# A graph layer's expert stage: final rows stored in node order, token gathers of one half row, scatters that add

## The chip, the cores and the metric
The kernel runs on one core of a Trainium2 chip. The metric is the device time of one execution in microseconds (us); the median of three runs of the kernel before is 795.6 us (794.12 to 796.25). All tensors are float32 unless a name says otherwise.

## The reference, cut to what matters
There are 3125 nodes with 256 features and 50000 edges sorted by destination. The function is one layer:

```python
xn = _layernorm(x)
x = x + _L0_gnn_ref(xn, src, dst, edge_type_8, ...) + _L0_mix_ref(xn[None], ...)[0]
x = x + _L0_ffn_ref(_layernorm(x)[None], ...)[0]
```

`_L0_gnn_ref` sums, for every node, the products of its edges' source rows with one of 8 relation matrices (each a mix of 4 bases), adds a loop product, applies GELU and a layer norm. `_L0_mix_ref` is a linear attention over all nodes. `_L0_ffn_ref` is a mixture of 32 experts with one expert per token:

```python
idx = jnp.argmax(logits, axis=-1)
h = relu(einsum('nd,ndh->nh', xf, W1[idx]) + b1[idx])      # 256 -> 64
out = relu(einsum('nh,nhd->nd', h, W2[idx]) + b2[idx])     # 64 -> 256
```

So each node has two rows of 256 numbers that the last stage needs: the row x after the first two parts (call it x2), and its normalised form, which the router and the experts read. The result is x2 plus the expert's output.

## The kernel before, in words
The nodes stand in NT = 25 tiles of 128 rows (the last has 53). Edges are worked in 49 "octets" of 8 x 128 edges. For each 128 edges GpSimd issues an indirect DMA (L534) that gathers 128 source rows of 1 KB from DRAM; TensorE multiplies them with a window matrix (L786), VectorE adds the products to an accumulator in SBUF (L1189). This is the edge stage, up to about 623 us. Its order is written out by hand in `edge_schedule`, and beside the later octets the node tiles are finished one by one (early and product on TensorE, gelu on ScalarE, first_stats, second_stats, finish_row and route on VectorE). `rowbuf` has three slots, and in each slot a tile's normalised rows lie in the first 256 columns and its x2 rows in the last 256.

`store_row(t)` on SyncE's queue (L409) waits until tile t's rows are ready (x2n_made) and stores the 512 columns to the DRAM tensor `rows_d` with one DMA. A slot is written again by tile t+3, for which VectorE waits on `stored`. On the same queue stand the loads of x (L404), the load of the experts' first weights (L413, L414) before the last tile's store, and that of the second weights (L418) after it.

The tail, after the last tile, is this. VectorE and TensorE sort the tokens by expert: `inv_i` gives for each place in sorted order the node that stands there (L1386 to L1436), and a table of NPAIR = 56 pairs (expert, token tile) says which tile each expert has tokens in. Then:
- GpSimd waits for all row stores and for inv_i, and issues 25 indirect gathers (L559), one for each tile of sorted tokens: 128 rows of 2 KB from `rows_d` into `token`, both halves.
- TensorE works in groups of 4 pairs, 14 groups. `hidden(g)` (L1025) is the first product, `turn_tiles(g + 1)` (L1015) transposes the next four token tiles once each has landed (f_in), `outer(g - 1)` (L1034) is the second product of the group before.
- ScalarE copies the four experts' weights of a group (load_w1, L711), applies ReLU to the hidden product once f_hid says it is there (L729), and copies the transposed tiles out of PSUM once f_turned says so (keep_turned, L718). hidden(g + 1) waits for these copies (f_xt).
- VectorE folds each pair's output into the tile's place in `f_ys` (L1482, one instruction a pair, counted by f_y). From pair 31 on, tile t = p - 31 is complete; `finish(t)` adds the gathered x2 half (L1473) and counts f_rows.
- GpSimd waits for f_rows and scatters the tile's 128 rows of 1 KB to `out` with an indirect DMA (L564). The last thing waited for is f_stored, all 25 scatters (SyncE).

A branch that is taken only for unusual edge lists (`redo`) repeats the work in a slower way; it isn't taken here.

Of the kernel before, what the change touches and what calls it, by code (L numbers as in the profile page):

```python
# [22 lines left out]
P = 128  # L23
N, D, E = 3125, 256, 50000
R, B, X, H = 8, 4, 32, 64
# [36 lines left out]
ALU = mybir.AluOpType  # L62
ACT = mybir.ActivationFunctionType
AX = mybir.AxisListType
F32, BF16 = mybir.dt.float32, mybir.dt.bfloat16
# [3 lines left out]
def rows(t):  # L69

    return P if t < NT - 1 else LAST
# [31 lines left out]
def gps_layer(nc, x, src_t, type_rows, dst_t, dst_rows, basis, comp, loop_w, h_bias, ln_gamma, ln_beta,  # L103
              w_qk, b_qk, w_v, b_v, bn_gamma, bn_beta, router_w, router_b, w1_t, b1_t, w2_t, relation_of,
              group_mask, out):
    with ExitStack() as ctx:
# [3 lines left out]
        def sem(name):  # L110
            return ctx.enter_context(nc.semaphore(name))
# [1 line left out]

        xn_d = nc.dram_tensor("xn_d", [N, D], F32).ap()
        bounds_d = nc.dram_tensor("bounds_d", [2, NWIN], I32).ap()
        rows_d = nc.dram_tensor("rows_d", [N, 2 * D], F32).ap()


        acc_raw = sb("acc_raw", [P, KD * B * NPAD])
# [6 lines left out]
        token = both[:, :].rearrange("p (t f) -> p t f", f=ROW)  # L126
# [70 lines left out]
        rowbuf = xn_raw[:, 8 * D:14 * D].rearrange("p (j f) -> p j f", j=3)  # L197
# [113 lines left out]
        once, again = Chain("once", v_own), Chain("again", Tally(sem("again_own")))  # L311
# [9 lines left out]
        f_in = [sem(f"f_in{s}") for s in range(NT)]  # L321
# [3 lines left out]
        f_relu = sem("f_relu")  # L325
        f_out = sem("f_out")
        f_y = sem("f_y")
        f_rows = sem("f_rows")
        f_w1 = sem("f_w1")
        f_stored = sem("f_stored")  # L330

# [38 lines left out]
        f_ys = acc_raw[:, at:at + NT * D]  # L370
# [35 lines left out]
        def store_row(eng, t, c):  # L406

            eng.wait_ge(c.x2n_made, t + 1)
            eng.dma_start(rows_d[t * P:t * P + rows(t), :], rowbuf[0:rows(t), t % 3, :]).then_inc(c.stored[t % 3], 16)  # L409

        def load_first(eng, done):

# [7 lines left out]
        def stores_of(j):  # L420

            return len(range(j, NT, 3))
# [72 lines left out]
        @block.gpsimd  # L495
        def _(pool):
            g = nc.gpsimd

            p_own.mark(g.memset(ident[:, :], 0.0))
            p_own.mark(g.memset(identb[:, :], 0.0))  # L500
            p_own.mark(g.memset(before[:, :], 1.0))
            g.memset(onesb[:, :], 1.0).then_inc(consts_made, 1)
            g.memset(ones_pp[:, :], 1.0).then_inc(consts_made, 1)
            at = p_own.mark(g.iota(part_i[:, :], pattern=[[0, 1]], base=0, channel_multiplier=1))
            pool.wait_ge(p_own.sem, at)
            g.tensor_copy(part_col[:, :], part_i[:, :]).then_inc(part_made, 1)
            at = p_own.mark(g.iota(iota_i[:, :], pattern=[[1, P]], base=0, channel_multiplier=0))
            for first, n, count in runs_of_reach():
                w = OCT // PAIR
                ins = g.iota(reach[:, first * w:(first + n) * w], pattern=[[P, n], [0, w]], base=P * count, channel_multiplier=0)  # L510
                p_own.mark(ins)
            pool.wait_ge(p_own.sem, p_own.at)
            pool.sem_inc(consts_made, 1)
            pool.wait_ge(p_own.sem, at)
            g.affine_select(out=ident[:, :], in_=ident[:, :], compare_op=ALU.not_equal, fill=1.0, base=0,
                            pattern=[[-1, P]], channel_multiplier=1).then_inc(consts_made, 1)
            g.affine_select(out=identb[:, :], in_=identb[:, :], compare_op=ALU.not_equal, fill=1.0, base=0,
                            pattern=[[-1, P]], channel_multiplier=1).then_inc(consts_made, 1)
            g.affine_select(out=before[:, :], in_=before[:, :], compare_op=ALU.is_gt, fill=0.0, base=0,
                            pattern=[[1, P]], channel_multiplier=-1).then_inc(consts_made, 1)  # L520
            g.tensor_copy(iota_b[:, :], iota_i[:, :]).then_inc(part_made, 1)
            pool.wait_ge(part_made, 2)
            g.tensor_copy(iota[:, :], iota_i[:, :]).then_inc(consts_made, 1)

            g.memset(acc_raw[:, TC * P:], 0.0).then_inc(acc_zeroed, 1)

            pool.wait_ge(xn_stored, 16 * (GROUPS + 1))
            pool.wait_ge(tables_loaded, 32)
            pool.wait_ge(rel_ready, 1)

            def octet(q, beside, i):
                for k in range(OCT):
                    pool.wait_ge(multiplied, OCT * q + k + 1)
                    g.indirect_dma_start(gath[:, k, :], None, xn_d,  # L534
                                         bass.IndirectOffsetOnAxis(ap=src_i[:, OCT * q + k:OCT * q + k + 1], axis=0)).then_inc(gathered[k], 16)

            edge_schedule(octet)


            pool.wait_ge(flag_ready, 1)  # L540
            redo = pool.value_load(flag[0:1, 0:1], min_val=0, max_val=1)
            with pool.If(redo > 0):
                with pool.Fori(0, NOCT * OCT) as t:
                    pool.wait_ge(slow_step, (2 * NT + 2) * t + 1)
                    g.tensor_copy(idx_st[:, 0:1], src_i[:, ds(t, 1)]).then_inc(slow_idx, 1)
                    pool.wait_ge(slow_idx, t + 1)
                    pool.sem_inc(slow_seen, 1)
                    g.indirect_dma_start(gath[:, 0, :], None, xn_d,
                                         bass.IndirectOffsetOnAxis(ap=idx_st[:, 0:1], axis=0)).then_inc(slow_gath, 16)
                    pool.wait_ge(slow_gath, 16 * t + 16)  # L550
                for j in range(3):
                    pool.wait_ge(again.stored[j], 16 * stores_of(j))

            for j in range(3):
                pool.wait_ge(once.stored[j], 16 * stores_of(j))
            pool.wait_ge(inv_ready, 1)
            for t in range(NT):
                n = rows(t)
                g.indirect_dma_start(token[0:n, t, 0:2 * D], None, rows_d,  # L559
                                     bass.IndirectOffsetOnAxis(ap=inv_i[0:n, t:t + 1], axis=0)).then_inc(f_in[t], 16)  # L560
            for t in range(NT):
                n = rows(t)
                pool.wait_ge(f_rows, t + 1)
                g.indirect_dma_start(out, bass.IndirectOffsetOnAxis(ap=inv_i[0:n, t:t + 1], axis=0),  # L564
                                     f_ys[0:n, t * D:(t + 1) * D], None).then_inc(f_stored, 16)


        @block.scalar
# [508 lines left out]
        def _(v):  # L1077
# [121 lines left out]
            def first_stats(t, c):  # L1199

                n = rows(t)
                v.wait_ge(c.gelu_done, t + 1)
                at = c.own.mark(d.bn_stats(stat_a[0:n, :], h[0:n, t % 2, :]))
                v.wait_ge(c.x_in[t % 3], 16 * (t // 3 + 1))
                if t >= 3:
                    v.wait_ge(c.stored[t % 3], 16 * (t // 3))
                c.own.mark(d.tensor_tensor(rowbuf[0:n, t % 3, D:2 * D], ps_mix[t % 2][0:n, D:2 * D], xr[0:n, t % 3, :], ALU.add))
                v.wait_ge(c.own.sem, at)
                d.bn_aggr(mv_a[0:n, :], stat_a[0:n, :]).then_inc(c.var_a, 1)
                v.wait_ge(c.var_a, t + 1)  # L1210
                d.scalar_tensor_tensor(y[0:n, :], h[0:n, t % 2, :], mv_a[0:n, 0:1], gam_bc[0:n, :], ALU.subtract, ALU.mult).then_inc(c.y_made, 1)
# [169 lines left out]
            def rank_and_experts(o):  # L1381
# [84 lines left out]

                d.memset(f_ys.bitcast(BF16), 0.0).then_inc(y_zeroed, 1)

                def finish(t):
                    n = rows(t)  # L1470
                    place = f_ys[0:n, t * D:(t + 1) * D]
                    v.wait_ge(f_in[t], 16)
                    d.tensor_tensor(place, place, token[0:n, t, D:2 * D], ALU.add).then_inc(f_rows, 1)  # L1473

                for g in range(NPAIR // FT):
                    tiles = row_values(v, pair_i[0:1, 1, FT * g:FT * (g + 1)], NT - 1, CLAMPED)
                    for f in range(FT):
                        p = FT * g + f
                        v.wait_ge(f_out, FT * g + f // 2 * 2 + 2)
                        v.wait_ge(f_y, p) if p > 0 else v.wait_ge(y_zeroed, 1)  # L1480
                        place = f_ys[:, ds(tiles[f] * D, D)]
                        d.scalar_tensor_tensor(place, ps[g % 2 * 2 + f // 2][:, f % 2 * D:(f % 2 + 1) * D], limit[:, p:p + 1], place, ALU.min, ALU.max).then_inc(f_y, 1)  # L1482
                        if p >= X - 1:
                            v.wait_ge(f_y, p + 1)
                            finish(p - X + 1)

            with v.If(redo < 1):
                rank_and_experts(v_own)
# [4 lines left out]
            with v.If(redo > 0):  # L1493
# [3 lines left out]
                v.wait_ge(ffn_loaded, 32)  # L1497
                v.wait_ge(w2_loaded, 16)
                for j in range(3):
                    v.wait_ge(once.stored[j], 16 * stores_of(j))  # L1500
                d.memset(acc_raw[:, :].bitcast(BF16), 0.0).then_inc(zero_again, 1)
                v.wait_ge(zero_again, 1)
                v.sem_inc(slow_step, 1)
# [78 lines left out]
```

## Time and profile before
| | us |
|---|---|
| median of 3 runs | 795.6 |
| profiled execution, its own time | 790.61 |
| its span in the trace | 788.7 |
| TensorE busy | 585.8 (74%) |
| VectorE busy | 386.3 (49%) |
| GpSimd busy | 458.2 (58%) |
| ScalarE busy | 163.5 (21%) |

One execution was recorded. PE is TensorE's matmuls, PEld its weight loads, DVE VectorE, ACT ScalarE, POOL GpSimd, SP SyncE; a q behind a name means that engine's instruction queue. "idle before <- X" is how long the engine had nothing to do before this group, and X is who ended it; "remote" stands where the profile finds no instruction that raised the awaited signal just then. The ends of matmuls are modelled. Numbers after a line's name are microseconds from the span's start, unless a column says ns.

### The profile page before, as it was taken

Reading aid. Unit: us, or ns where it says so; the run is one execution under the profiler, and the core shown is the slowest. Engines: PE = TensorE matmul, PEld = TensorE weight load, DVE = VectorE, ACT = ScalarE, POOL = GpSimd, SP = SyncE. Lnnn points to the kernel's source line nnn. Section 1 sums busy time; section 2 is a strip of 40 time slices with the busy share of each in tenths; the row PEclk is TensorE's granted clock in tenths of the full one; section 3 lists DMA queues with packets and bytes.
Section 4 is the critical chain, followed back from the end, with each engine's and each line's share of the span. In section 5 each row is a group of like instructions: output and inputs, shape, how many; then the busy total and the mean of one; then the engine's idle time right before and its main releaser. Section 6 shows DMA issues by size and latency. Waiting matters only on the chain.

```text
span 788.7 us, 10440 instructions
## 1 busy us (share of the span) xinstructions
PE 585.8 (74%) x3181; PEld 471.6 (60%) x3181; DVE 386.3 (49%) x1272; ACT 163.5 (21%) x345; POOL 458.2 (58%) x464
## 2 busy tenths in 40 slices
PE   0366686888888768698999798897979982419980
PEld 0356675666665647477777666775858741318860
DVE  2844445333322334446666646456547677303552
ACT  0450000000000001022332312132122350115520
POOL 9146676666666666566676667666666400740165
PEclk9969999898999998699999888899989995559986
DMA  8563333333333344234434433334334326640021
GB/s 227 157 185 88 87 99 88 90 89 91 93 91 94 91 141 121 68 94 126 123 115 131 126 112 115 103 114 128 110 108 130 108 99 166 200 126 2 15 81 72
DMA packets 41872, 86.78 MB, mean 110 GB/s; under 512 B 11280, under 2 KB 23378, under 8 KB 41491
## 3 DMA queue, kind: packets, MB, share of 16 engines
q0 software_dynamic: 22576, 61.01, 26.7%
q1 hardware_dynamic: 18372, 22.95, 9.4%
q10 hardware_dynamic: 864, 2.08, 1.1%
q8 instruction: 29, 0.48, 0.2%
q14 instruction: 31, 0.25, 0.1%
HBM read 73.21 MB, written 12.80 MB: 109 GB/s over the span
## 4 chain that ended last, share of the span: by engine, by line
PE 56%; another core or an unknown queue 14%; DVE 10%; issue 7%; DMA 4%; POOL 3%; ACT 2%; SPq 1%; DVEq 0%; ACTq 0%; POOLq 0%
PE ps L786 23%; PE ps L828 11%; PE ps L817 6%; PE ps L1025 3%; PE ps L1034 2%; PE ps L793 2%; DMA both<-in_x 2%; PE ps L800 2%; POOL gath L534 2%; PE ps L805 2%; DMA gath<-xn_d,src_i 1%; POOL out L564 1%; PE ps L850 1%; PE ps L840 1%
## 5 line engine op out<-in xcount | busy, mean ns | idle before, releaser
L534 POOL DMA_INDIRECT gath<-xn_d,src_i x392 | 386.5, 986 | 214.9 <-issue 90.9
L786 PE MATMUL ps<-wmat,gath 128*128 128x144 f32 x1568 | 257.8, 309 | 25.5 <-DMA gath<-xn_d,src_i 10.7
L786 PEld LDWEIGHTS ps<-wmat,gath 128*128 128x128 f32 x1568 | 229.4, 203 | 50.8 <-issue 22.4
L1189 DVE TENSOR_TENSOR acc_raw<-acc_raw,ps 128x144 f32 x392 | 101.8, 300 | 283.2 <-PE ps L786 203.5
L1162 DVE TENSOR_TENSOR wmat<-hit,wts 128x576 f32<-128x576 f32 x100 | 75.3, 753 | 0.3
L564 POOL DMA_INDIRECT out<-acc_raw,inv_i x25 | 25.4, 1015 | 55.5 <-DVE acc_raw L1473 49.1
L1482 DVE SCALAR_TENSOR_TENSOR acc_raw<-ps,wts,acc_raw 128x256 f32 x56 | 27.0, 482 | 59.7 <-PE ps L1034 46.6
L559 POOL DMA_INDIRECT both<-rows_d,inv_i x25 | 24.3, 971 | 52.6 <-DVE inv_i L1436 45.2
L828 PE MATMUL ps<-wk_et,acc_raw 128*128 128x256 f32 (+1 forms) x200 | 53.1, 391 | 0.0
L828 PE MATMUL ps<-wq_wv,acc_raw 128*128 128x256 f32 (+1 forms) x200 | 52.6, 388 | 0.0
L817 PE MATMUL ps<-cmat,both 128*128 128x512 f32 (+1 forms) x100 | 52.5, 651 | 0.0
L1025 PE MATMUL ps<-acc_raw,gath 128*64 x224 | 33.3, 308 | 24.9 <-ACT acc_raw L718 22.7
L1025 PEld LDWEIGHTS ps<-acc_raw,gath 128*64 128x64 f32 x224 | 28.8, 156 | 30.7 <-issue 30.7
L793 PE MATMUL ps<-both,wk_et 128*128 128x256 f32 (+1 forms) x104 | 29.9, 414 | 18.4 <-DVE top L1197 18.4
L828 PEld LDWEIGHTS ps<-wq_wv,acc_raw 128*128 128x128 f32 (+1 forms) x200 | 36.9, 193 | 4.8 <-issue 0.2
L805 PE MATMUL ps<-both,wk_et 128*128 128x257 f32 (+1 forms) x100 | 28.5, 410 | 14.8 <-ACT wk_et L621 7.8
L828 PEld LDWEIGHTS ps<-wk_et,acc_raw 128*128 128x128 f32 (+1 forms) x200 | 35.1, 194 | 3.6 <-issue 0.2
L621 ACT ACTIVATE wk_et<-ps 128x256 f32<-128x256 f32 x24 | 9.2, 384 | 126.9 <-remote 71.3
L840 PE MATMUL ps<-ident,both 128*128 128x128 f32 (+1 forms) x50 | 11.2, 308 | 31.4 <-issue 16.4
L750 PE MATMUL ps<-ident,both 128*128 128x128 f32 x50 | 10.8, 387 | 31.6 <-DVEq L1116 23.7
L793 PEld LDWEIGHTS ps<-both,wk_et 128*128 128x128 f32 x104 | 19.6, 210 | 21.8 <-DVE top L1197 19.6
L646 ACT ACT_TABLE_LOAD x25 | 32.1, 1283 | 0.5
(194 smaller groups left out, 619.7 us busy)
## 6 DMA issues: line engine op xcount, KB each, us to landing
gath<-xn_d,src_i POOLq DMA_INDIRECT x392
rows_d<-both SPq DMA_DIRECT2D x24, 256.0 KB
both<-in_x SPq DMA_DIRECT2D x24, 128.0 KB
both<-in_x SPq DMA_DIRECT2D x4, 640.0 KB, 17.2
xn_d<-both SPq DMA_DIRECT2D x4, 640.0 KB
acc_raw<-in_w_t SPq DMA_DIRECT2D x1, 2080.0 KB
acc_raw<-in_w_t SPq DMA_DIRECT2D x1, 2048.0 KB, 7.5
acc_raw<-in_type_rows ACTq DMA_DIRECT2D x1, 1600.0 KB, 15.6
```

The lines of the kernel that those rows point to most:

```text
L534: g.indirect_dma_start(gath[:, k, :], None, xn_d, bass.IndirectOffsetOnAxis(ap=src_i[:, OCT * q + k:OCT * q + k + 1], axis=0)).then_inc(ga ...
L564: g.indirect_dma_start(out, bass.IndirectOffsetOnAxis(ap=inv_i[0:n, t:t + 1], axis=0), f_ys[0:n, t * D:(t + 1) * D], None).then_inc(f_stor ...
L646: s.activation(h[0:n, t % 2, :], ps_mix[t % 2][0:n, 0:D], ACT.Gelu).then_inc(c.gelu_done, 1)
L786: ins = t_.matmul(ps_edge[quarter][:, m * B * WIN:(m + 1) * B * WIN], gath[:, k, m * P:(m + 1) * P], wmat[:, k, :, :].rearrange("p b w -> ...
L793: ins = t_.matmul(ps_mix[m][:, 0:n], wk[:, k, m * P:(m + 1) * P], xnt[:, k, ds(first, n)], start=k == 0, stop=k == KD - 1)
L805: ins = t_.matmul(ps_sum[m][:, 0:D + 1], et[0:n, j, m * P:(m + 1) * P], tile, start=start, stop=stop)
L817: t_.matmul(bank, xnt[:, k, P * t:P * t + n], cmat[:, k, :], start=k == 0, stop=False)
L828: ins = t_.matmul(ps_mix[t % 2][0:n, 0:D], acc[:, f, t * P:t * P + n], basis_sb[m][:, b, :], start=False, stop=f == KD * B - 1, skip_group ...
L1025: ins = t_.matmul(ps[4 + g % 2][0:H, f * P:(f + 1) * P], f_w[:, g % 2, f, k * H:(k + 1) * H], xts[:, ds(tiles[f] * D + k * P, P)], start=k ...
L1162: d.tensor_tensor(wmat[:, half * w:half * w + w, :, :], hit[:, :, :].unsqueeze(2).to_broadcast([P, w, B, WIN]), wts[:, :, cut].rearrange(" ...
L1189: d.tensor_tensor(place, place, ps_edge[w][:, m * B * WIN:(m + 1) * B * WIN].rearrange("p (b w) -> p b w", w=WIN), ALU.add).then_inc(added, 1)
L1482: d.scalar_tensor_tensor(place, ps[g % 2 * 2 + f // 2][:, f % 2 * D:(f % 2 + 1) * D], limit[:, p:p + 1], place, ALU.min, ALU.max).then_inc ...
```

## The change
Each tile is stored with two DMAs: the normalised half to `rows_d`, which now has 256 columns, and the x2 half straight to its node rows of `out`. The gathers fetch only the normalised half, 1 KB a row. VectorE's finish is gone, and the scatter of tile t waits for f_y >= t + 32 (the fold of pair t + 31). The scatter is an accumulating DMA: it adds the rows of `f_ys` to what lies in `out`. The waits on `stored` count 32 a tile, as two DMAs raise it by 16 each.

```diff
-        rows_d = nc.dram_tensor("rows_d", [N, 2 * D], F32).ap()
+        rows_d = nc.dram_tensor("rows_d", [N, D], F32).ap()
...
             eng.wait_ge(c.x2n_made, t + 1)
-            eng.dma_start(rows_d[t * P:t * P + rows(t), :], rowbuf[0:rows(t), t % 3, :]).then_inc(c.stored[t % 3], 16)
+            eng.dma_start(rows_d[t * P:t * P + rows(t), :], rowbuf[0:rows(t), t % 3, 0:D]).then_inc(c.stored[t % 3], 16)
+            eng.dma_start(out[t * P:t * P + rows(t), :], rowbuf[0:rows(t), t % 3, D:2 * D]).then_inc(c.stored[t % 3], 16)
...
             for j in range(3):
-                pool.wait_ge(once.stored[j], 16 * stores_of(j))
+                pool.wait_ge(once.stored[j], 32 * stores_of(j))
             pool.wait_ge(inv_ready, 1)
             for t in range(NT):
                 n = rows(t)
-                g.indirect_dma_start(token[0:n, t, 0:2 * D], None, rows_d,
+                g.indirect_dma_start(token[0:n, t, 0:D], None, rows_d,
                                      bass.IndirectOffsetOnAxis(ap=inv_i[0:n, t:t + 1], axis=0)).then_inc(f_in[t], 16)
             for t in range(NT):
                 n = rows(t)
-                pool.wait_ge(f_rows, t + 1)
+                pool.wait_ge(f_y, t + X)
                 g.indirect_dma_start(out, bass.IndirectOffsetOnAxis(ap=inv_i[0:n, t:t + 1], axis=0),
-                                     f_ys[0:n, t * D:(t + 1) * D], None).then_inc(f_stored, 16)
+                                     f_ys[0:n, t * D:(t + 1) * D], None, compute_op=ALU.add).then_inc(f_stored, 16)
...
                 if t >= 3:
-                    v.wait_ge(c.stored[t % 3], 16 * (t // 3))
+                    v.wait_ge(c.stored[t % 3], 32 * (t // 3))
...
-                def finish(t):
-                    n = rows(t)
-                    place = f_ys[0:n, t * D:(t + 1) * D]
-                    v.wait_ge(f_in[t], 16)
-                    d.tensor_tensor(place, place, token[0:n, t, D:2 * D], ALU.add).then_inc(f_rows, 1)
...
                         d.scalar_tensor_tensor(place, ps[g % 2 * 2 + f // 2][:, f % 2 * D:(f % 2 + 1) * D], limit[:, p:p + 1], place, ALU.min, ALU.max).then_inc(f_y, 1)
-                        if p >= X - 1:
-                            v.wait_ge(f_y, p + 1)
-                            finish(p - X + 1)
```

## Rows read from the trace of the kernel before
**Rows 1.** Busy time by stretch, core 0: microseconds and counts; last clock, DMA share, GB/s.
```profile
102.00:600.00 498.00, 412.97 (x2197) 332.01 (x2196) 241.15 (x841) 85.48 (x142) 333.68 (x338) 0.92 0.36 107
671.00:701.00 30.00, 9.11 (x34) 6.64 (x34) 7.25 (x7) 3.89 (x14) 22.99 (x24) 0.56 0.72 206
712.00:745.00 33.00, 33.00 (x219) 27.70 (x217) 15.48 (x32) 17.71 (x68) 0.00 (x0) 1.00 0.01 1
761.40:782.30 20.90, 8.97 (x37) 7.07 (x35) 11.50 (x27) 1.68 (x7) 16.28 (x16) 0.66 0.24 97
783.30:785.80 2.50, 0.00 (x0) 0.00 (x0) 0.00 (x0) 0.00 (x0) 0.00 (x0) 0.50 0.08 21
```
**Rows 2.** Chain of waits, end of the kernel: start, length, what.
```profile
678.88 18.28 another core or an unknown queue
```
**Rows 3.** Timeline while the tokens are gathered: start, length, engine, line, idle before.
```profile
652.33 0.24 SPq L409 DMA_DIRECT2D rows_d<-both  x1
...
669.75 0.94 POOL L559 DMA_INDIRECT both<-rows_d,inv_i  x1 [45.25 <-DVE inv_i L1436]
...
679.03 3.67 PE L1025 MATMUL ps<-acc_raw,gath 128*64 x16 [1.11 <-ACT acc_raw L718]
...
682.63 1.97 PE L1015 MATMUL ps<-ident,both 128*128 128x128 f32 x8
...
697.28 1.12 ACT L729 ACTIVATE gath<-ps,acc_raw 64x128 f32<-64x128 f32 x4 [18.40 <-remote]
...
704.93 1.07 ACT L718 COPY acc_raw<-ps 128x512 f32<-128x512 f32 x2 [6.53 <-remote]
...
706.15 3.67 PE L1025 MATMUL ps<-acc_raw,gath 128*64 x16 [21.56 <-ACT acc_raw L718]
```
**Rows 4.** Timeline after the gathers, while GpSimd is silent.
```profile
713.56 1.96 PE L1025 MATMUL ps<-acc_raw,gath 128*64 x16
...
715.66 1.12 ACT L729 ACTIVATE gath<-ps,acc_raw 64x128 f32<-64x128 f32 x4 [2.46 <-PE ps L1025]
...
716.38 1.89 PE L1034 MATMUL ps<-acc_raw,gath 65*128 x8
...
718.21 1.96 PE L1025 MATMUL ps<-acc_raw,gath 128*64 x16
```
**Rows 5.** The two indirect transfers of the tail: shortest, median, longest in ns.
```profile
L559 POOL DMA_INDIRECT both<-rows_d,inv_i x25: 942/947/1573, 669.7 to 699.8; - x25
...
L564 POOL DMA_INDIRECT out<-acc_raw,inv_i x25: 967/972/1557, 745.7 to 780.7; - x25
```
**Rows 6.** Timeline of the scatters.
```profile
745.01 0.42 DVE L1473 TENSOR_TENSOR acc_raw<-acc_raw,both 128x256 f32<-128x256 f32 x1
...
745.71 1.03 POOL L564 DMA_INDIRECT out<-acc_raw,inv_i  x1 [44.37 <-DVE acc_raw L1473]
...
752.53 1.99 PE L1034 MATMUL ps<-acc_raw,gath 65*128 x8
...
759.13 0.48 DVE L1482 SCALAR_TENSOR_TENSOR acc_raw<-ps,wts,acc_raw 128x256 f32 x1 [4.09 <-remote]
...
759.54 3.60 PE L1034 MATMUL ps<-acc_raw,gath 65*128 x8 [0.19 <-ACT gath L729]
...
761.38 0.97 POOL L564 DMA_INDIRECT out<-acc_raw,inv_i  x1 [3.79 <-DVE acc_raw L1473]
...
766.65 3.72 PE L1034 MATMUL ps<-acc_raw,gath 65*128 x16
...
776.47 0.48 DVE L1482 SCALAR_TENSOR_TENSOR acc_raw<-ps,wts,acc_raw 128x256 f32 x1 [3.00 <-remote]
...
780.69 1.56 POOL L564 DMA_INDIRECT out<-acc_raw,inv_i  x1 [0.30 <-issue]
```
**Rows 7.** Who waited for whom, edge stage: total, times, longest.
```profile
DVE acc_raw L1189 <- PE ps L786: 187.8, 88, 5.9
...
DVE acc_raw L1189 <- remote: 59.5, 29, 3.6
```

More of the change, by code:

```diff
@@ L327, in gps_layer @@
         f_y = sem("f_y")
-        f_rows = sem("f_rows")
         f_w1 = sem("f_w1")
@@ L551, in _ @@
                 for j in range(3):
-                    pool.wait_ge(again.stored[j], 16 * stores_of(j))
+                    pool.wait_ge(again.stored[j], 32 * stores_of(j))
             for j in range(3):
-                pool.wait_ge(once.stored[j], 16 * stores_of(j))
+                pool.wait_ge(once.stored[j], 32 * stores_of(j))
             pool.wait_ge(inv_ready, 1)
@@ L1499, in _ @@
                 for j in range(3):
-                    v.wait_ge(once.stored[j], 16 * stores_of(j))
+                    v.wait_ge(once.stored[j], 32 * stores_of(j))
                 d.memset(acc_raw[:, :].bitcast(BF16), 0.0).then_inc(zero_again, 1)
```

## The prediction, on record before the changed kernel ran
> **What bounds the kernel now.** I read the page's slices first: in the tail the DMA digits are high while TensorE is nearly idle. Then busy time by stretch. The edge stage is TensorE's (413 of 498 us busy), and the change leaves its instructions alone. From 671 to 701 us TensorE is busy for 9 us of 30, GpSimd for 23, and the DMA engines move 206 GB/s at a share of 0.72: this is the gather of the tokens. From 712 to 745 us TensorE is busy all the time at the full granted clock (1.0, 2.4 GHz). From 761.4 to 782.3 us GpSimd's scatters fill the stretch (16.3 of 20.9 us busy) [rows 1].
>
> The chain of waits has one link of 18.28 us from 678.88, called unknown [rows 2]. In the timeline it is ScalarE, which starts the ReLU of group 0 at 697.28 after 18.40 us of idle, though TensorE's hidden(0) stands as ended at 682.70 and the transposes behind it at 684.60. A second wait ends at 704.93 with the copies out of PSUM, for transposes that also ended at 684.60. So TensorE's signals arrive 14.6 and up to 20.3 us late, and hidden(1) starts only at 706.15 [rows 3]. With GpSimd silent there is no such lag: hidden(2) ends at 715.52 and its ReLU starts at 715.66 [rows 4]. While GpSimd scatters there is one again, but shorter: the outer product ends at 754.52 and VectorE's fold starts at 759.13; the one that ends at 770.37 is folded at 776.47 [rows 6]. In the edge stage, with 1 KB gathers at most times, VectorE's longest idle before its additions is 5.9 us, and 3.6 where nothing else explains it [rows 7]; that bounds a lag there from above, for the idle holds true waiting too. I read this as: TensorE's completion signals are held back while indirect DMAs run, for 3 to 6 us where rows have 1 KB, for 15 to 20 us where they have 2 KB. That the size of the row makes the difference is the assumption of this forecast; the number of DMAs in a row would be another reading.
>
> **The change, part by part.**
>
> *Two stores for one.* SyncE issues one more DMA a tile; the last store's issue took 0.24 us at 652.33. The bytes are the same. All stores must have landed before the first gather, which starts at 669.75 and waits for inv_i [rows 3]: 17 us of cover. The weights' loads behind them slip by one issue, some 0.3 us, against first uses past 670 us. The slots' second use is three tiles later. I take 0. Were the cover gone, it would cost the landing of one store.
>
> *Gathers of 1 KB.* The issue is not cheaper: 947 ns for 2 KB rows, and 972 ns for the 1 KB rows of the scatter [rows 5]. 25 of them at 0.947 + 0.30 of gap fill 31 us, as now. A tile can't be there earlier than now by more than its shorter transfer, and tile t is issued at 669.75 + 1.25 t. What changes is the traffic: 206 GB/s would halve to about 103, near the 107 of the edge stage and the 97 of the scatters [rows 1]. So I give TensorE's signals a lag of 4 us in place of 14.6 (between 3.6 and 5.9 of [rows 7]). Then: ReLU of group 0 at 682.7 + 4 = 686.7; it takes 1.12, the copies behind it 1.22 until hidden starts (704.93 to 706.15): hidden(1) at 689.0. It takes 3.67, the transposes 1.97 [rows 3]. f_hid arrives at 692.7 + 4 = 696.7, and with 1.12 + 1.22 hidden(2) starts at 699.0, TensorE's own work (3.67 + 1.97 + 3.60 for the outer product at the lower clock [rows 6]) ending at 698.3. Then 3.67 + 1.97 + 3.60 again: hidden(3) at 708.3. Now it starts at 718.21 [rows 4]. That is 9.9 us, less a little because the granted clock rose to 1.0 only by 712 and may be late again: I take -9.5. Bounds: 0, if the lag stays until the gathers end; -14.7, if there is none (hidden(1) at 685.0, then two times 9.24: hidden(3) at 703.5, and the clock may well be up earlier, so up to -16).
>
> A rule of the Trainium skill speaks against this. "DMA: Bandwidth & Descriptors", section "Anatomy of one DMA — SWDGE (gpsimd) path", gives a transfer issued by GpSimd about 2 us of fixed cost plus bytes over 436 GB/s, so 1 KB rows save 0.3 us of a gather and nothing of its issue. By it this part would be worth 0.3 us; what it leaves out is the lag of TensorE's signals that the rows show.
>
> *finish is gone.* The first scatter waits now for a fold and a finish of 0.42 us that starts at 745.01; it starts at 745.71 [rows 6]. -0.4. The other 24 are hidden behind GpSimd's stream.
>
> *Scatters that add.* Now: 745.71 to 782.25 (780.69 + 1.56) are 36.5 us for 25 issues; at 0.972 + 0.30 with the longer last one they would be 32.4, and the rest is the gap of 3.79 us before 761.38, a late signal [rows 5, 6]. No row shows an accumulating DMA. From below: the plain scatter, 972 ns. From above: the 1557 ns of the longest of these issues, and, further off, twice the plain one, 1.94 us, if every row needs a second address worked out. I take +0.2 us an issue, nearer to the plain row, since the index and the row count are the same: +5.0 over 25, of which the gap absorbs 1.8 (nine slower scatters come later to it): +3.2. Bounds 0 and +14.9 - 3.8 = +11 (1557 ns), +24.4 - 3.8 = +20.6 (1.94 us). Behind the last issue the trace has 6.45 us to the end of the span, in 2.5 of which the DMA share is 0.08, a little over one engine of 16 (0.0625) [rows 1]: the 53 rows of the last tile go through one engine. If the add needs a second read for each row, these 2.5 us may double. +2.0, bounds 0 and +2.5. The other scatters' transfers have room: a share of 0.24 in the stream [rows 1].
>
> "Collectives: The Full Stack", section "The bandwidth ceiling: the fold count and why AG ≠ RS ≠ AR", of the Trainium skill says that an add in the DMA path costs two source reads and two reading descriptors a chunk, which halved the rate there. By it the last tile would pay all of its 2.5 us, and GpSimd would have half as many descriptors more to write, 1.46 us an issue for 0.972: +12.2 - 3.8 = +8.4 for the stream. No run here shows it.
>
> *Sum* against the profiled execution: 0 - 9.5 - 0.4 + 3.2 + 2.0 = -4.7, so a span of 784.0 and a time of 785.9. The median of the runs lies 5.0 us above the profiled time; I carry that over: 795.6 - 4.7 = **790.9 us**.
>
> **The rivals.**
> 1. *The signals stay held until the gathers end.* The gathers are as many and as dense as before, and if it is their issue and not their bytes that holds the signals, hidden(1) starts near 704 to 706 as now. For it: the scatters too have 1 KB rows and lags of 4 to 6 us at a share of 0.24. Against: these are a third of 14.6 to 20.3. Price: the -9.5 falls away, +4.8 stays: 800.4 us.
> 2. *GpSimd's scatters become the end*, the other side. The mechanism: an accumulating issue is dear, and from 745 on GpSimd's stream is what ends last, so each 0.1 us costs 2.5. At 1557 ns: -9.9 + 11.1 + 2.5 = +3.7, 799.3 us; at 1.94 us: -9.9 + 20.6 + 2.5 = +13.2, 808.8 us. It decides from where 25 e - 3.8 + 2.5 exceeds 9.9, e = 0.45: an issue of 1.42 us. For it: the stream is full already. Against: issues of the same row count cost the same for one and two KB and for both directions.
> 3. *No lag and a plain price.* TensorE follows the gathers, and the scatter costs as now: -14.7 - 0.4 = -15.1, 780.5 us. For it: the lag in the edge stage is short most of the time.
>
> **How the numbers follow.** Forecast 0.43 (its own range 786 to 796), rival 1 0.22, rival 2 0.20, rival 3 0.15. About 0.3% (2.4 us) is what a measurement of this kernel can tell from no change. Faster: 0.36 of the forecast, all of rival 3, 0.03 of rival 1, 0.01 of rival 2: 0.55. Slower: 0.15 of rival 1, 0.17 of rival 2, 0.02 of the forecast: 0.34. The same: 0.11. Range 781 to 806: it leaves out half of rival 3 and the dear end of rival 2.
>
> **What would show it.** Right: ReLU of group 0 within 6 us of hidden(0)'s end, hidden(3) at 705 to 711, a DMA share near 0.4 in the gathers; L564 at 1.0 to 1.35 us; 7 to 9 us from the last issue to the end. Wrong: the 18.4 us idle before L729 still there (rival 1); L564 at 1.4 us or more and no gap left in its stream (rival 2). A wait on `stored` that ends after inv_i would make the two stores dear; I see none.

## The result: 810.9 us, 2% slower, and outside the range

The changed kernel took 810.86 us (median of 4 runs, 808.19 to 813.27), the kernel before 795.13 us on the same chip (794.12 to 796.25): a ratio of 1.0197, 95% interval 1.016 to 1.0233. The forecast was 790.9 us, the range 781 to 806.

The two profiled executions lie at opposite ends of what the runs show: before at 790.61 with a median of 795.13, after at 813.27 with a median of 810.86. So the traces differ by 22.7 us and the timed runs by 15.7. A part of the trace's difference, 9.5 us, is already there when the first gather starts (669.75 before, 679.26 after), ahead of everything that the prediction priced but the two stores; in two later profiles of the same pair (e5, e6 below) the last gathers are 1.2 us apart (698.90 and 697.68). The stretches are therefore measured from the first gather.

The tail of the changed kernel. The chain of waits, its links from 687.15 on that are over 2 us long (start, length, what):
```profile
687.15 21.04 issue
709.42 5.16 another core or an unknown queue x2
715.79 3.67 PE ps L1025 x16
799.71 2.75 POOL out L564
```
The same stretch in the timeline (start, length, engine, line, idle before):
```profile
679.26 0.94 POOL L559 DMA_INDIRECT both<-rows_d,inv_i  x1 [44.95 <-DVE inv_i L1436]
...
687.30 3.67 PE L1025 MATMUL ps<-acc_raw,gath 128*64 x16 [0.83 <-ACT acc_raw L718]
...
690.90 1.13 PE L1015 MATMUL ps<-ident,both 128*128 128x128 f32 x8
...
708.30 1.12 ACT L729 ACTIVATE gath<-ps,acc_raw 64x128 f32<-64x128 f32 x4 [21.14 <-issue]
709.21 1.57 POOL L559 DMA_INDIRECT both<-rows_d,inv_i  x1 [0.30 <-issue]
714.57 1.07 ACT L718 COPY acc_raw<-ps 128x512 f32<-128x512 f32 x2 [5.15 <-remote]
715.79 3.67 PE L1025 MATMUL ps<-acc_raw,gath 128*64 x16 [23.77 <-ACT acc_raw L718]
...
754.96 1.65 POOL L564 DMA_INDIRECT out<-acc_raw,inv_i  x1 [44.18 <-DVE acc_raw L1476]
...
756.91 1.58 POOL L564 DMA_INDIRECT out<-acc_raw,inv_i  x1 [0.31 <-issue]
...
799.71 2.75 POOL L564 DMA_INDIRECT out<-acc_raw,inv_i  x1 [0.30 <-issue]
```
This answers to [rows 3] and [rows 6]. ScalarE is idle for 21.14 us before the ReLU of group 0, where before it was 18.40: hidden(0) stands as ended at 690.97 and its signal arrives at 708.30, when GpSimd is about to issue its last gather. Nothing of the expected gain is there. From the first gather to the first scatter it is 75.96 us before and 75.70 after. From the first scatter to the end of the last issue it is 36.5 us before and 47.5 after, and behind that 6.45 and 8.9 us to the end of the span.

The two indirect transfers of the changed kernel (shortest, median, longest in ns), against [rows 5]:
```profile
L559 POOL DMA_INDIRECT both<-rows_d,inv_i x25: 942/944/1572, 679.3 to 709.2; - x25
...
L564 POOL DMA_INDIRECT out<-acc_raw,inv_i x25: 1553/1553/2750, 755.0 to 799.7; - x25
```
Busy time by stretch (as in [rows 1]: PE, PEld, DVE, ACT, POOL busy; clock, DMA share, GB/s): the gathers, the second half of the scatters, and what lies behind the last issue:
```profile
681.00:711.00 30.00, 7.61 (x34) 5.77 (x33) 7.15 (x6) 3.85 (x14) 22.78 (x24) 0.56 0.36 104
771.00:802.40 31.40, 2.58 (x12) 1.92 (x11) 3.87 (x8) 0.18 (x1) 26.52 (x17) 0.59 0.62 70
802.50:805.00 2.50, 0.00 (x0) 0.00 (x0) 0.00 (x0) 0.00 (x0) 0.00 (x0) 0.50 0.21 8
805.00:808.00 3.00, 0.00 (x0) 0.00 (x0) 0.00 (x0) 0.00 (x0) 0.00 (x0) 0.50 0.08 12
```
The traffic of the gathers did halve (206 to 104 GB/s, share 0.72 to 0.36), as the prediction said, and TensorE is no busier for it (7.61 us in 30, before 9.11). The adding scatters keep the DMA engines busier (share 0.62, before 0.24) while they move less (70 GB/s, before 97).

### The profile page after: what moved, and what is told of

Its sections match the earlier page's. It is cut to its first block, busy times and chain, and to the rows that moved or that the text cites. A ratio compares the mean times of both kernels' runs of the same rounds, so it can differ in the third digit from the quotient of the medians.

```text
span 811.4 us, 10414 instructions
## 1 busy us (share of the span) xinstructions
PE 584.2 (72%) x3180; PEld 470.0 (58%) x3181; DVE 377.7 (47%) x1247; ACT 163.6 (20%) x345; POOL 470.6 (58%) x464
## 4 chain that ended last, share of the span: by engine, by line
PE 50%; another core or an unknown queue 17%; issue 11%; DVE 9%; POOL 5%; DMA 3%; ACT 3%; SPq 1%; DVEq 0%; POOLq 0%; ACTq 0%
PE ps L786 19%; PE ps L828 10%; PE ps L817 6%; PE ps L1025 3%; POOL out L564 3%; PE ps L1034 3%; PE ps L793 3%; DMA both<-in_x 2%; POOL gath L534 2%; PE ps L850 1%; PE ps L840 1%; DVE acc_raw L1189 1%; PE ps L818 1%; ACT wk_et L621 1%
## 5 line engine op out<-in xcount | busy, mean ns | idle before, releaser
L786 PE MATMUL ps<-wmat,gath 128*128 128x144 f32 x1568 | 260.9, 310 | 28.6 <-DMA gath<-xn_d,src_i 10.9
L564 POOL DMA_INDIRECT out<-acc_raw,inv_i x25 | 40.2, 1607 | 51.5 <-DVE acc_raw L1476 46.6
L828 PE MATMUL ps<-wk_et,acc_raw 128*128 128x256 f32 (+1 forms) x200 | 51.3, 380 | 0.0
L1025 PE MATMUL ps<-acc_raw,gath 128*64 x224 | 30.9, 297 | 24.6 <-ACT acc_raw L718 24.6
L840 PE MATMUL ps<-ident,both 128*128 128x128 f32 (+1 forms) x50 | 10.9, 302 | 36.5 <-issue 28.0
L658 ACT ACTIVATE both<-both,eps_col 128x1 f32<-128x1 f32 (+1 forms) x25 | 7.4, 295 | 124.7 <-DVE both L1225 75.4
L646 ACT ACT_TABLE_LOAD x25 | 32.1, 1283 | 0.4
L1152 DVE TENSOR_TENSOR hit<-rel,iota 128x144 f32<-128x144 f32 x100 | 30.3, 303 | 3.1 <-ACT wts L599 3.1
```

The source lines that it names most:

```text
L646: s.activation(h[0:n, t % 2, :], ps_mix[t % 2][0:n, 0:D], ACT.Gelu).then_inc(c.gelu_done, 1)
L786: ins = t_.matmul(ps_edge[quarter][:, m * B * WIN:(m + 1) * B * WIN], gath[:, k, m * P:(m + 1) * P], wmat[:, k, :, :].rearrange("p b w -> ...
L828: ins = t_.matmul(ps_mix[t % 2][0:n, 0:D], acc[:, f, t * P:t * P + n], basis_sb[m][:, b, :], start=False, stop=f == KD * B - 1, skip_group ...
L1025: ins = t_.matmul(ps[4 + g % 2][0:H, f * P:(f + 1) * P], f_w[:, g % 2, f, k * H:(k + 1) * H], xts[:, ds(tiles[f] * D + k * P, P)], start=k ...
L1152: d.tensor_tensor(hit[:, :, :], rel[:, cut].unsqueeze(2).to_broadcast([P, w, WIN]), iota[:, 0:WIN].unsqueeze(1).to_broadcast([P, w, WIN]), ...
```

## The experiments

The chips that ran these kernels are of two sorts, and each experiment can only be read with that. The kernel before took 795.1 us on the chip of the first measurement (its number isn't on record), 692.6 on that of e1 to e4, 789.5 (e5 to e8), 692.8 (e9 to e12) and 799.0 (e13 to e15); the last four are different chips. In the traces of the two chips near 692 us TensorE's signals arrive on time ("punctual" below); in those of the others they are late. "Late" is read against the end of the matmuls, which the profile models; the same model gives 0.14 us on a punctual chip (e2), so the difference between chips is real, but whether the matmuls end late or their signals are held can't be seen. Each ratio is to the kernel before on the same chip.

**On a punctual chip.**

*e1, two stores alone.* The kernel before, its row store cut in two DMAs to the same tensor:
```diff
-            eng.dma_start(rows_d[t * P:t * P + rows(t), :], rowbuf[0:rows(t), t % 3, :]).then_inc(c.stored[t % 3], 16)
+            eng.dma_start(rows_d[t * P:t * P + rows(t), 0:D], rowbuf[0:rows(t), t % 3, 0:D]).then_inc(c.stored[t % 3], 16)
+            eng.dma_start(rows_d[t * P:t * P + rows(t), D:2 * D], rowbuf[0:rows(t), t % 3, D:2 * D]).then_inc(c.stored[t % 3], 16)
```


> The kernel before with each tile's row store cut into two DMAs of 1 KB rows (both halves still go to rows_d, gathers, finish and scatters as before). Theory A (the two stores cost nothing, all 15.7 us lie in the tail): 795.1, within 1 us of before. Theory B (they slow the later edge stage, since the profile of the change has its first gather 9.5 us later, of which 3.6 stood before the first store): 797 to 801.

691.22 us, ratio 0.9987 (0.996 to 1.0015). The second store costs nothing that can be measured.

*e2, the change without the add.* Its scatters overwrite, so the x2 half is missing from the output.
```diff
-                                     f_ys[0:n, t * D:(t + 1) * D], None, compute_op=ALU.add).then_inc(f_stored, 16)
+                                     f_ys[0:n, t * D:(t + 1) * D], None).then_inc(f_stored, 16)
```


> The changed kernel with scatters that overwrite instead of adding (the add of x2 is left out). Theory A (the accumulating issue is the whole loss): L564 back at 0.97 us, 8.9 us behind the last issue back to 6.4, late signals in the scatters again, so 13 us faster than the change: 796 to 798. Rival (GpSimd's stream is long for another reason, the two stores or the bytes): 803 or more.

687.25 us, ratio 0.9935 (0.9911 to 0.9959): 5.3 us of gain, and not by way of TensorE's signals. The timeline of e2, hidden(0) and its ReLU:
```profile
601.89 3.67 PE L1025 MATMUL ps<-acc_raw,gath 128*64 x16 [0.83 <-ACT acc_raw L718]
...
605.70 1.12 ACT L729 ACTIVATE gath<-ps,acc_raw 64x128 f32<-64x128 f32 x4 [3.96 <-PE ps L1025]
```
The ReLU starts 0.14 us after hidden(0), though GpSimd issues its gathers just as densely. There is no lag on this chip, and from the first gather (593.82) to the first scatter (645.92) it takes 52.1 us where it took 75.7. What the smaller rows gain here is the wait for the tiles themselves: TensorE's transposes wait for gathered tiles for 5.2 us in all in e1 (2 KB rows) and for 1.1 us in e2, and e1 takes 56.3 us from the first gather to the first scatter.

*e3, pauses in the gathers.* The kernel before with one wait more, so that GpSimd issues 12 gathers and then four at a time, each four once the tiles up to four back are transposed:
```diff
             for t in range(NT):
                 n = rows(t)
+                if t >= 3 * FT and t % FT == 0:
+                    pool.wait_ge(f_turned, t - FT)
```


> The kernel before, with GpSimd's gathers paced: tiles 12, 16, 20 and 24 each wait until TensorE's transposes of all but the four tiles before them are counted. Theory I (an unbroken run of GpSimd's indirect DMAs holds TensorE's signals, whatever their bytes; a pause lets them out): the 18.4 us idle before L729 shrinks to 3 to 7, group 3's hidden product starts near 708 in place of 718, 785 to 789. Rival (the signals are late for a reason that has nothing to do with the gathers' run, or the gathers' end is what counts): 795, or slower by the pauses, 797.

692.24 us, ratio 1.0013 (0.9985 to 1.0041). Where no signal is late, pauses gain nothing and cost nothing.

*e4, GpSimd silent.* The changed kernel with its gathers replaced by plain loads on SyncE's queue, in node order; the sort is left out of the loads:
```diff
+            sp.wait_ge(inv_ready, 1)
+            for t in range(NT):
+                sp.dma_start(token[0:rows(t), t, 0:D], rows_d[t * P:t * P + rows(t), :]).then_inc(f_in[t], 16)
...
-                g.indirect_dma_start(token[0:n, t, 0:D], None, rows_d,
-                                     bass.IndirectOffsetOnAxis(ap=inv_i[0:n, t:t + 1], axis=0)).then_inc(f_in[t], 16)
```


> The changed kernel with the 25 token loads issued by SyncE as direct DMAs of the same 128 KB, in node order (the sort of the tokens is left out). Theory I (GpSimd's issues hold TensorE's signals): ReLU of group 0 starts within 1 us of its product's end, group 3 starts 15 to 20 us earlier after inv_i, the accumulating scatters stay: 791 to 796. Rival (any DMA traffic into the token buffer holds them): the long idle stays, 809 to 811.

706.05 us, ratio 1.0192 (1.0157 to 1.0227). The change with its own gathers was not run on this chip, so what the loads gain here can't be read from this run; the accumulating scatters (median 1553 ns) make it slower than e2.

**On a chip with late signals (before 789.5 us).**

*e5 and e6, the pair again.* The changed kernel and the kernel before, unaltered.

> The changed kernel once more, beside the kernel before, on the chip of this comparison. Where TensorE's signals are on time (as in the four runs before, 692.6 for the kernel before): the overwriting form was 5.3 us faster than before, the add costs 25 x 0.58 + 2.5 = 17 us, so 704, 12 us slower than before (ratio 1.017). Where they are late: 811 against 795, as first measured. Rival (on such a chip the stream starts so much earlier that the add is covered): ratio under 1.005.

> The kernel before, for its profile on the chip of this comparison. If TensorE's signals are on time: ReLU of group 0 starts within 0.3 us of its product's end, the edge stage ends some 75 us earlier than in the first profile, 690 to 694. If late: 791 to 796 with the 18 us idle before L729.

e5: 804.66 us, ratio 1.0193 (1.0167 to 1.0218), the first result again; e6: 788.07 us. From the timelines, first e5, then e6:
```profile
676.87 3.67 PE L1025 MATMUL ps<-acc_raw,gath 128*64 x16 [0.83 <-ACT acc_raw L718]
...
692.83 1.12 ACT L729 ACTIVATE gath<-ps,acc_raw 64x128 f32<-64x128 f32 x4 [16.10 <-remote]
...
698.90 1.58 POOL L559 DMA_INDIRECT both<-rows_d,inv_i  x1 [0.30 <-issue]
...
742.60 1.65 POOL L564 DMA_INDIRECT out<-acc_raw,inv_i  x1 [42.13 <-DVE acc_raw L1476]
...
787.38 2.75 POOL L564 DMA_INDIRECT out<-acc_raw,inv_i  x1 [0.30 <-issue]
```
```profile
676.98 3.67 PE L1025 MATMUL ps<-acc_raw,gath 128*64 x16 [1.12 <-issue]
...
694.48 1.12 ACT L729 ACTIVATE gath<-ps,acc_raw 64x128 f32<-64x128 f32 x4 [17.65 <-remote]
...
697.68 1.57 POOL L559 DMA_INDIRECT both<-rows_d,inv_i  x1 [0.30 <-issue]
...
743.12 1.02 POOL L564 DMA_INDIRECT out<-acc_raw,inv_i  x1 [43.86 <-DVE acc_raw L1473]
...
778.14 1.56 POOL L564 DMA_INDIRECT out<-acc_raw,inv_i  x1 [0.30 <-issue]
```
The first scatters start within 0.5 us of one another, the last 9.2 us apart. With 1.2 us more for the last issue and 2.5 behind it that is the whole 12.9 us between the spans (786.2 and 799.1). This pair compares the two row sizes on one chip: with half the bytes hidden(0)'s signal is 12.3 us late, with all of them 13.8, and from the first gather to the first scatter it takes 73.7 us in place of 75.4. In both the signal arrives while GpSimd is still issuing (7.6 and 4.8 us before the last gather's issue ends), so it isn't held until the run of issues is over.

*e7, fewer rows to add.* The changed kernel; each accumulating scatter carries at most 64 rows, the other rows are left out:
```diff
             for t in range(NT):
                 n = rows(t)
+                n = min(n, 64)
                 pool.wait_ge(f_y, t + X)
```


> The changed kernel with each accumulating scatter cut to its first 64 rows (the other rows' adds are left out). Theory D (the add costs GpSimd per row, since it writes more for each): L564 falls from 1.55 to 1.0 us or less. Rival (a fixed extra of 0.58 us for an accumulating DMA): L564 at 1.4 to 1.55 us.

803.46 us in one run. The scatters of e7:
```profile
L565 POOL DMA_INDIRECT out<-acc_raw,inv_i x25: 1397/1401/2762, 749.0 to 790.0; - x25
```
Half of the rows take 0.15 us off 1.55, and 64 added rows still cost 0.43 us more than 128 plain ones. The reading that each row's second address makes the price would give 1.26 us (0.972 and half of 0.58). The larger part of the price doesn't go by the rows, then, provided that a plain scatter of 64 rows costs no more than one of 128; that was not run. The last tile's 53 rows are dearest in every version.

*e8, pauses in the kernel before.* The edit of e3.

> The paced gathers of the run before, once more, for a chip on which TensorE's signals are late. There theory I (an unbroken run of GpSimd's DMAs holds them) expects 6 to 10 us less than before and an idle of 3 to 7 us before L729. Where signals are on time, both theories expect no change (ratio 0.998 to 1.003).

775.86 us, ratio **0.9819** (0.9795 to 0.9843): faster than both kernels, by 13.6 us over the kernel before. The timeline of e8 while the tokens are gathered:
```profile
683.71 0.95 POOL L561 DMA_INDIRECT both<-rows_d,inv_i  x1 [0.30 <-issue]
686.97 1.12 ACT L731 ACTIVATE gath<-ps,acc_raw 64x128 f32<-64x128 f32 x4 [7.91 <-remote]
687.27 0.94 POOL L561 DMA_INDIRECT both<-rows_d,inv_i  x1 [2.61 <-remote]
...
689.18 3.67 PE L1027 MATMUL ps<-acc_raw,gath 128*64 x16 [5.09 <-ACT acc_raw L720]
...
691.02 0.95 POOL L561 DMA_INDIRECT both<-rows_d,inv_i  x1 [0.30 <-issue]
...
692.99 1.12 ACT L731 ACTIVATE gath<-ps,acc_raw 64x128 f32<-64x128 f32 x4 [3.16 <-PE ps L1027]
...
707.13 1.57 POOL L561 DMA_INDIRECT both<-rows_d,inv_i  x1 [1.90 <-PE ps L1017]
...
731.57 1.03 POOL L566 DMA_INDIRECT out<-acc_raw,inv_i  x1 [22.87 <-DVE acc_raw L1475]
```
GpSimd stops issuing at 684.66 (683.71 + 0.95); 2.3 us later ScalarE receives TensorE's signal, and 2.6 us later GpSimd. The idle before the ReLU falls from 17.65 to 7.91 us. The last gather is issued 9.5 us later than in e6 (707.13 for 697.68), and the first scatter 11.6 us earlier. The gain is more than was expected (6 to 10 us), though the idle stayed longer than the 3 to 7 us that the expectation had.

**On another punctual chip (before 692.8 us).** These four were meant for late signals, and the chip had none; so e10 and e11 only repeat e2 and e4.

> The changed kernel, with one wait more: before the gathers of tiles 12, 16, 20 and 24 GpSimd waits until the tiles up to four back are transposed, so that its issues come in bursts. Theory (an unbroken run of GpSimd's indirect issues holds TensorE's signals; the bytes of the rows do not matter): where the kernel before takes some 790 us, the pauses give the change the 13.6 us that they gave the kernel before, so about 1.002 of before (1.019 - 0.017): the idle before the ReLU of group 0 falls from 16 to 8 us, first scatter some 11 us earlier. Rival (the gain of the pauses came from the 2 KB rows' traffic, which 1 KB rows do not have): still 1.019. Where TensorE's signals are on time anyway (before near 692 us) both expect 1.019 and nothing is told apart.

The change with the pauses of e3: 705.88 us, ratio 1.0202 (1.0138 to 1.0267). The change without pauses was not run on a punctual chip; e11 below, without GpSimd's gathers, takes the same time.

> The changed kernel without the add (its scatters overwrite, so the x2 half is missing from the output). Theory (bytes of the gathered rows do not matter, the accumulating issue costs 0.58 us more): where signals are late, idle before the ReLU of group 0 is 16 to 18 us as before, first scatter within 1 us of before, ratio 0.995 to 1.000. Rival (bytes do matter, and the first pair of profiles hid it in run-to-run variation): idle of 4 to 8 us and ratio 0.98 to 0.988. Against the change (1.019) both expect the add alone to be worth 15 to 19 us where nothing else changes: 11 of issues, 1.2 of the last issue, 2.5 of landing, and the late-signal gap it covers.

The kernel of e2: 687.38 us, ratio 0.9926 (0.9892 to 0.996). Against e9 that is 18.5 us for the add, more than on a late chip, since here no gap of late signals takes up a part of it.

> The changed kernel with the 25 token gathers replaced by plain loads of 25 x 128 rows in node order on SyncE's queue (the sort by expert is left out, so tokens meet wrong experts; all counts and sizes stay). GpSimd is silent, the bytes and the 25 waits are the same. Theory (GpSimd's issuing holds the signals): ReLU of group 0 starts within 3 us of hidden(0)'s end, first scatter 14 to 17 us earlier than in the change, ratio 1.000 to 1.004 where before is some 790 us. Rival (the transfers' traffic, or something of this place in the program, holds them): idle of 10 us or more remains, ratio 1.012 to 1.019. Where signals are on time: 1.019, as measured once.

The kernel of e4: 705.56 us, ratio 1.0187 (1.0122 to 1.0252).

> The kernel before with pauses that begin one group earlier: the gathers of tiles 8, 12, 16, 20 and 24 wait. Theory: 8 issues in a row in place of 12 (10 us in place of 15), so the idle before the ReLU of group 0 falls from 7.9 to 2 to 4 us; the later groups are bound by their own chain, so 2 to 5 us less than the version that pauses from tile 12: 0.976 to 0.980. Rival (the pauses now starve TensorE of tiles, since each group waits for the last transposes of the one before): 0.982 to 0.988. Where signals are on time: 1.000 to 1.006, the pauses can only cost.

The edit of e3 with `t >= 2 * FT`: 693.29 us, ratio 1.0028 (0.9992 to 1.0064). Whether the earlier pause gains anything where signals are late was not tried.

**On another chip with late signals (before 799.0 us).**

> The changed kernel without the add (the x2 half is missing from the output), once more, since the last chip had TensorE's signals on time. Expected only for a chip where they are late (before some 790 us). Theory (bytes of the gathered rows do not matter): idle of 16 to 18 us before the ReLU of group 0 as in before, first scatter within 1 us of before, ratio 0.995 to 1.000. Rival (bytes do matter): idle of 4 to 8 us and ratio 0.98 to 0.988. On a chip with punctual signals: 0.993, as twice.

The kernel of e2: 797.12 us, ratio 0.9981 (0.9962 to 1.0001). The timeline, and the scatters:
```profile
705.95 1.12 ACT L729 ACTIVATE gath<-ps,acc_raw 64x128 f32<-64x128 f32 x4 [21.23 <-issue]
706.83 1.57 POOL L559 DMA_INDIRECT both<-rows_d,inv_i  x1 [0.30 <-issue]
712.25 1.07 ACT L718 COPY acc_raw<-ps 128x512 f32<-128x512 f32 x2 [5.17 <-remote]
```
```profile
L564 POOL DMA_INDIRECT out<-acc_raw,inv_i x25: 969/974/1560, 752.2 to 787.5; - x25
```
Rows of 1 KB, a plain scatter, and the long idle is there in full. All of the change but the add is worth 1.9 us here, at the edge of what can be told from nothing.

> The changed kernel with the 25 token gathers replaced by plain loads on SyncE's queue in node order (the sort is left out of the loads), once more for a chip with late signals. Theory (GpSimd's issuing holds the signals): ReLU of group 0 starts within 3 us of hidden(0)'s end, first scatter 14 to 17 us earlier than in the change, ratio 1.000 to 1.004. Rival (the traffic or the place in the program): idle of 10 us or more, 1.012 to 1.019. On a chip with punctual signals: 1.019, as twice.

The kernel of e4, GpSimd silent: 787.24 us, ratio **0.9866** (0.9827 to 0.9905), although its scatters cost 1555 ns as in the change. The timeline, and the stretch of the loads:
```profile
675.88 11.58 SPq L496 DMA_DIRECT2D both<-rows_d  x25
...
684.53 3.67 PE L1026 MATMUL ps<-acc_raw,gath 128*64 x16 [0.91 <-ACT acc_raw L719]
...
688.34 1.12 ACT L730 ACTIVATE gath<-ps,acc_raw 64x128 f32<-64x128 f32 x4 [3.96 <-PE ps L1026]
...
690.57 1.96 PE L1026 MATMUL ps<-acc_raw,gath 128*64 x16 [1.34 <-ACT acc_raw L719]
...
695.21 1.96 PE L1026 MATMUL ps<-acc_raw,gath 128*64 x16
```
```profile
677.00:688.00 11.00, 6.52 (x26) 5.34 (x26) 7.88 (x11) 2.66 (x10) 0.00 (x0) 0.50 0.86 257
```
The DMA engines move 257 GB/s at a share of 0.86 (206 and 0.72 in the gathers of the kernel before), and the ReLU starts 0.14 us after hidden(0). So it is not the traffic that makes TensorE's signals late. The loads differ from the gathers in two things, though: SyncE issues them, and they are not indirect. Which of the two frees the signals this run doesn't tell. From the first load to the first scatter (727.50) it takes 51.6 us, in place of 75.7. The expectation (1.000 to 1.004) was too high, in the main because it valued the lag at 14 to 17 us where it is worth 24.

> The changed kernel with pauses before the gathers of tiles 12, 16, 20 and 24, once more for a chip with late signals. Theory (an unbroken run of issues holds the signals): 1.002, idle before the ReLU of group 0 near 8 us. Rival (the pauses helped only because of the 2 KB rows' traffic): 1.019. On a chip with punctual signals: 1.020, as once.

The kernel of e9: 796.22 us, ratio 0.9968 (0.9943 to 0.9993). The pauses take the change from 2% slower to a little faster than before, where 1.002 was expected. The change without them was not run on this chip (1.0193 and 1.0197 in the other two sessions with late signals); against e13, on this chip, the first scatter comes 61.7 us after the first gather in place of 75.5. The idle before its first ReLU:
```profile
693.66 1.12 ACT L731 ACTIVATE gath<-ps,acc_raw 64x128 f32<-64x128 f32 x4 [9.39 <-remote]
```

## Why the prediction was wrong

*Two stores, 0.* Right as far as the runs go: e1 on a punctual chip, and on a late one e13, which has both stores and is no slower than the kernel before. By themselves they were not run on a late chip.

*Gathers of 1 KB, -9.5.* Wrong, and with it the sign of the sum. The step that failed is the assumption that "the size of the row makes the difference": the lag was read off two stages that differ in three things, the rows' size, the traffic and how densely GpSimd issues, and I gave it to the first. The runs took the size apart from the rest: with half the bytes the idle stays (21.14 us in the change, 21.23 in e13, and 16.10 beside 17.65 in e5 and e6, on one chip), with more traffic and no indirect gather of GpSimd it is gone (e14), with the same DMAs in bursts it is more than halved (e8). On these chips the late signals go with GpSimd's dense indirect gathers, 25 in a row at 1.25 us each, whatever their rows' size; whether it is the issuing or the transfers' form, and what lets the signals through before the run is over, stays open. Measured worth of the smaller rows with finish gone: -1.9 us at a late chip (e13), -5.3 and -5.5 at the punctual ones (e2, e10), by the medians. Rival 1 named this and had 0.22; its argument, 25 issues as dense as before, stood in the text. The bound was off too: the whole lag is worth 24 us (75.7 less 51.6), where I had put no more than 16. The step that fell short is the clock: without the lag I had hidden(1) at 685.0, 15.3 us after the first gather (14.7 in e14), but then two groups at 9.24 us each, at the lower clock. In e14 a group takes 4.64 us (690.57 to 695.21) and the granted clock is 1.00 from 688 to 700 us, so hidden(3) comes 9.2 us earlier still.

The rule that I weighed and set aside, in the Trainium skill's "DMA: Bandwidth & Descriptors", section "Anatomy of one DMA — SWDGE (gpsimd) path" (a fixed cost plus a small term for bytes), gave 0.3 us for this part. It speaks of the time until the transfer has landed, and there the traces show a larger difference: 3.6 us from issue to landing before, 2.7 in the change (medians), so 0.9 us saved for each gather. The issue stayed the same, 944 ns for 947. As the forecast of this part 0.3 us was close on the late chips, because the tiles' landing is not what TensorE waits for there; on a punctual chip it is, and the smaller rows gained more (e2).

*finish is gone, -0.4.* It can't be told apart in the timed runs; in the first pair of profiles the first scatter comes 0.26 us earlier after the first gather, in e5 and e6 1.7 us, smaller rows and finish together.

*Scatters that add, +3.2.* The mechanism was right and the size wrong: an issue costs 1.553 us, not 1.17. 24 x 0.58 and 1.19 for the last are 15.1 us, of which the gap of late signals absorbed 4.1, as the prediction had it do (3.8): +11.0, the bound that the text had at 1557 ns. (Two of its sums are off by 0.3 us: 25 issues at 0.585 us more are 14.6, not 14.9, and the stream without a gap is 32.1 us by its terms, not 32.4; the punctual chips show 32.6 to 32.8. Neither changes a conclusion.) I had taken the value near the plain row because the index and the row count were the same; e7 suggests that rows are the smaller part of it. *Last landing, +2.0*: measured +2.5, the bound.

The other rule, in the Trainium skill's "Collectives: The Full Stack", section "The bandwidth ceiling: the fold count and why AG ≠ RS ≠ AR" (an add in the DMA path costs two source reads), gave as I worked it out an estimate of 1.46 us an issue and the full 2.5 for the landing. The trace has 1.553 us and 2.5. GpSimd's queue carries 2928 packets more than without the add, for the same bytes (packets, MB, share of 16 engines; the change, then e13):
```profile
q0 software_dynamic: 24528, 57.82, 27.1%
```
```profile
q0 software_dynamic: 21600, 57.81, 25.0%
```
In e7, which scatters 1536 rows fewer, it carries 1536 packets fewer (22992). The packets go by the rows, but e7 does not bear out that the issue's price does, which was my reading of that rule. Both rules together would have given 795.6 - 0.3 - 0.4 + 8.4 + 2.5 = 805.8 us.

With the measured terms the sum is 795.6 + 0 + 0 - 0.3 + 11.0 + 2.5 = 808.8 us, within the runs of the changed kernel (808.19 to 813.27) and 2.1 us under their median. From the first gather on the two traces differ by 13.2 us, the medians by 15.7; where the rest lies no run shows. (Rival 2 had the same 808.8 at 1.94 us an issue; that is chance, for it kept the gain of the gathers and had a price that was not measured.) The result is rivals 1 and 2 at once: no gain in the gathers, and GpSimd's scatters as the end. I had them as alternatives and gave their joint case no chance. From the prediction's own terms it could be had: 790.61 - 0.4 + 11.1 + 2.5 + 5.0 = 808.8, beyond the range.

*What stays open.* Why a chip shows the lag and another doesn't. Where the other 75 us between the two sorts of chips arise: that is how much earlier the first gather starts on a punctual one (594.58 in e1, 669.75 before), so it lies ahead of the tail, in stages that were not experimented on. The edge stage's waits for signals that nothing explains, there in the late chips' traces and not in e1's ([rows 7], and the last section), point to the same lag; that is argued, not shown.

## What to carry to other kernels

Before a transfer is made smaller, ask of the wait beside it what else differs between the stages where it is long and short, and change one of these things by itself; here, on chips with late signals, two lines that let GpSimd pause were worth 1.8% and half the bytes next to nothing. An add in an indirect DMA is not free: on a path where GpSimd issues back to back it must be priced by the issue, and VectorE's 0.42 us that it replaced was hidden. Two rivals that can both be true need a joint case in the range.

## What the runs showed of the hardware

- TensorE's signals reach ScalarE 12 to 23 us after the modelled ends of matmuls and transposes (692.83 for 680.54 in e5; 708.30 for 690.97 and 714.57 for 692.03 in the change) beside GpSimd's 25 dense indirect gathers, on the chips where the kernel before takes 789 to 799 us. The signal of hidden(0) arrives before the gathers' issues end; that of the transposes 3.8 us after the last issue in the change. In e8 the signal is there 2.3 us after GpSimd stops. On the two punctual chips they arrive within 0.2 us under the same stream. In the edge stage of the kernel before VectorE has 29 waits for a signal that nothing explains ([rows 7]); e1's trace, on a punctual chip, has none of them. Its waits of VectorE before the additions from 102 to 560 us (total, times, longest):
```profile
DVE acc_raw L1190 <- PE ps L787: 180.0, 120, 4.1
DVE acc_raw L1190 <- issue: 2.3, 6, 0.4
```
- One program takes 692.6 us on one chip and 799.0 on another, with no more than 1% between the runs on one chip's median and its extremes. A ratio has to be taken on one chip, and the pauses show that it can also depend on the chip: 0.9819 at one with late signals, 1.0013 at a punctual one.
- An accumulating indirect DMA of 128 rows of 1 KB takes GpSimd 1.553 us to issue, a plain one 0.972. With 64 rows it is 1.401; the last one, 53 rows, takes 2.75 for 1.56.
